# Graph network on one core: 19 and 21 of 64 tiles of source rows by matmul instead of 23 and 24

## What is computed

```python
w = relu(edgefeats @ w1 + b1) @ w2 + b2          # 400000 x 256, once
W = w.reshape(-1, 16, 16)
for _ in range(2):
    xj = hx[edge_src]                            # source rows, gathered anew in each round
    m = einsum('ei,eio->eo', xj, W)
    agg = segment_sum(m, edge_dst) / max(deg, 1)
    hx = gru_cell(agg, hx)
out = layernorm(x + hx)
```

## Time and profile before

| | |
|---|---|
| median of three runs | 6714.77 us |
| span of the profiled execution | 6694.6 us |
| around the span (median less span) | 20.2 us |
| PE busy | 5648.0 us (84%), 38360 matmuls |
| DVE busy | 4296.9 us (64%) |
| POOL busy | 3811.1 us (57%), 4006 gathers |
| ACT busy | 3179.0 us (47%) |
| granted TensorE clock, mean | 0.882 of 2.4 GHz |

### The profile page before, as it was taken

The page is one execution under the profiler, slowest core; times in us unless marked ns, Lnnn a source line. Parts: engine busy times, 40 slices in busy tenths (PEclk is TensorE's granted clock), DMA queues, the critical chain, the costliest instruction groups (busy, mean ns, idle before and its releaser), DMA issues.

```text
span 6694.6 us, 119595 instructions
## 1 busy us (share of the span) xinstructions
PE 5648.0 (84%) x38360; PEld 4666.6 (70%) x38361; DVE 4296.9 (64%) x7146; ACT 3179.0 (47%) x5259; POOL 3811.1 (57%) x4021
## 2 busy tenths in 40 slices
PE   2888888888888888888858888888888888888887
PEld 1777777777777777777647777776777777777775
DVE  3766666666666666666636666666666666666665
ACT  1554555445554545454325454454545454444442
POOL 6355555555555555555555555555555555555553
PEclk7988998889898999998878898898988889888887
DMA  4111111111111111111111111111111111111110
GB/s 107 46 34 48 34 48 34 48 34 48 34 48 44 39 48 34 48 34 48 25 47 29 40 29 40 33 37 39 31 40 29 40 29 41 29 40 29 40 29 20
DMA packets 197656, 263.32 MB, mean 39 GB/s; under 512 B 95745, under 2 KB 165942, under 8 KB 184205
## 3 DMA queue, kind: packets, MB, share of 16 engines
q1 hardware_dynamic: 61885, 216.66, 9.5%
q0 software_dynamic: 128192, 33.07, 4.8%
q10 hardware_dynamic: 7026, 6.21, 0.4%
HBM read 195.73 MB, written 54.92 MB: 37 GB/s over the span
## 4 chain that ended last, share of the span: by engine, by line
PE 65%; issue 14%; another core or an unknown queue 10%; ACT 6%; DVE 3%; DVEq 1%; DMA 0%; POOL 0%; ACTq 0%; POOLq 0%; SPq 0%
PE ps_all L722 45%; PE ps_all L732 8%; ACT src_hot L603 3%; PE ps_all L755 3%; PE ps_all L745 3%; PE ps_all L709 3%; PE ps_all L776 2%; ACT src_hot L607 2%; DVE shared L1137 1%; DVE fan L1092 1%; PE ps_all L762 0%; ACT shared L576 0%; ACT h_sb L570 0%; DVE xg L1145 0%
## 5 line engine op out<-in xcount | busy, mean ns | idle before, releaser
L722 PE MATMUL ps_all<-parts,src_hot 125*128 125x400 f32 x18048 | 3820.4, 368 | 258.7 <-issue 166.4
L722 PEld LDWEIGHTS ps_all<-parts,src_hot 125*128 125x128 f32 x18048 | 3501.9, 202 | 482.6 <-issue 367.7
L535 POOL DMA_INDIRECT xg<-in_x,idx x2027 | 1923.4, 949 | 1394.3 <-issue 556.1
L535 POOL DMA_INDIRECT xg<-h_rows,idx x1979 | 1873.1, 946 | 1371.6 <-issue 518.7
L1137 DVE TENSOR_TENSOR shared<-ps_all,at_hot 128x400 f32<-128x400 f32 x2256 | 1211.8, 566 | 1858.8 <-remote 1168.4
L603 ACT ACTIVATE src_hot<-keys,neg_key 128x384 fp32r<-128x384 int16 (+1 forms) x3072 | 1617.0, 599 | 1653.1 <-remote 979.0
L732 PE MATMUL ps_all<-fan,h_sb 128*32 128x160 f32 x12544 | 825.0, 316 | 489.5 <-issue 435.8
L1092 DVE TENSOR_TENSOR fan<-xg,ps_all 128x1280 f32<-128x1280 f32 x784 | 1158.8, 1478 | 88.0 <-DVE xg L1145 33.4
L607 ACT ACTIVATE src_hot<-src_hot 128x1536 fp32r<-128x1536 f32 (+1 forms) x768 | 1122.2, 1461 | 72.3 <-ACT src_hot L603 2.8
L1145 DVE TENSOR_REDUCE xg<-shared 128x48 f32<-128x1200 f32 (+1 forms) x768 | 1056.7, 1376 | 75.6 <-DVE shared L1137 1.0
L732 PEld LDWEIGHTS ps_all<-fan,h_sb 128*32 128x32 f32 x12544 | 391.8, 111 | 842.4 <-issue 794.9
(11 more groups left out here) (120 smaller groups left out, 1383.7 us busy)
## 6 DMA issues: line engine op xcount, KB each, us to landing
keys<-key_d SPq DMA_DIRECT2D x96, 768.0 KB
h_d<-h_sb SPq DMA_DIRECT2D x49, 1056.0 KB
h_sb<-h_d SPq DMA_DIRECT2D x49, 1056.0 KB
xg<-in_x,idx POOLq DMA_INDIRECT x2027
xg<-h_rows,idx POOLq DMA_INDIRECT x1979
ef<-in_ef_t SPq DMA_DIRECT2D x49, 420.0 KB
acc_all<-agg_t SPq DMA_DIRECT2D x1, 3161.0 KB
idx<-in_src_tiles SPq DMA_DIRECT2D x98, 32.0 KB
```

The costliest lines, as they stand in the source:

```text
L535: pool.indirect_dma_start(out=xg[:, buf, at, 0:C], out_offset=None, in_=rows_of, in_offset=bass.IndirectOffsetOnAxis(ap=idx[:, buf, at:at ...
L722: last = pe.matmul(ps_g[j], src_hot[0:KP, k % 2, kb, j * P:(j + 1) * P], parts[0:KP, m, kb, :], start=(kb == 0 and m == 0), stop=(kb == KB ...
```

## The change

Two rows of numbers. In round 0 steps 1, 2, 4 and 6 go from 3 tiles by PE to 2 (sum 23 to 19). In round 1 steps 0, 1 and 4 do (24 to 21). POOL gathers 45 and 43 tiles of a super instead of 41 and 40. The buffers and tables of `keys`, `at_pe` and `at_hot`, sized by the larger number of each step, shrink from 24 tiles to 21.

```diff
-BY_PE = ((2, 3, 3, 3, 3, 3, 3, 3), (3, 3, 3, 3, 3, 3, 3, 3))
+BY_PE = ((2, 2, 2, 3, 2, 3, 2, 3), (2, 2, 3, 3, 2, 3, 3, 3))
```

## The result

The changed kernel takes 6956.9 us, median of 4 runs (6954.7 to 6963.8), against 6715.4 us, median of 4 runs of the kernel before: ratio 1.0371, 95% interval 1.0348 to 1.0394. Forecast was 6215 us. It is slower by 242 us, not faster by 500.

What follows compares the result with a forecast made beforehand. PE with its stutters was taken to bound the kernel; -530 (tiles) -20 (ACT) +40 (DVE) +10 (round starts) gave -500 us, so 6215 us from 6715, with a range of 6110 to 6450 us.

Steps and rivals of the forecast that it cites:

- I put the steady state at nothing: POOL's 336 added gathers, 420 us more work, were to hide in its idle time and cost 0 us.
- The free step boundary of rows 6: On POOL, a step boundary was read to cost nothing when its wait is already fulfilled: the same 0.30 us of idle.
- PE with its stutters sets the pace: PE, 84% busy and stuttering with no named wait, was taken as the bound on a super of about 66 us.
- -530 us for the tiles: PE loses 4 and 3 tiles a super over 47 supers in each round: 510 to 555 us gained, taken as 530.
- +40 and -20 us of hand-offs: 40 us lost to PE's waits for DVE's picks, 20 us gained from shorter waits for ACT's one-hots.
- The cover of 24 us for each gather: Gathers run 24 us ahead of the PE products that use their rows, so one more gather, 1.25 us, was covered.
- Slower: POOL already sets the pace: Rival, chance 0.06: POOL's own step cost fills its idle time, so added gathers cost 411 us: 7126 us.
- the 376 waits: POOL's waits for an update of unknown maker, 782.9 us in all, taken as waits for PE's `products`.
- Price by number: Rival, chance 0.18: PE's instructions cost by number, about 84 ns each: 6273 us; a skill-page price gave 326 us saved.
- hand-offs: Rival, chance 0.13: half of the 500 us returns as waits for picks and one-hots: 6465 us; sign, over 150 us.
- more gained: Rival, chance 0.10: PE's stutters fall with its instruction count, 65 us, plus the tiles' upper end: about 6115 us.
- L722 at 15360: Sign of being right: 15360 PE matmuls on that line, a super about 60 us, POOL's waits for PE some 700 us.

Runs made afterwards that it cites:

- long set: Runs on one chip where the kernel before, unedited, takes 6712 to 6761 us (medians).
- y3_no_gathers: Kernel before, but from super 2 on POOL issues no gathers (those rows are left out of the sums): 5170.0 us, ratio 0.7708.
- short sets: The two sets of runs, each on its own chip, where the kernel before, unedited, takes 5146 and 5151 us.
- x4_lead8: Kernel before with LEAD 8 instead of 4, where the kernel before takes about 5.15 ms: 5144.3 us, ratio 0.9997.
- z3_pause: Kernel before, but POOL waits after every step until its own gathers have landed: 6928.7 us, ratio 1.0254.

## Why the prediction was wrong

**The step that failed: "I put the steady state at nothing"** for 336 added gathers. Alone they cost 447 us in a long set and 415 us in a short one: 1.33 and 1.24 us each, where gathers back to back start 1.25 us apart. The arithmetic took POOL's 14.8 us idle in a super for free room. It is not free: it is eight pauses of about 2 us, one behind every burst, and a longer burst does not eat its pause but lengthens it (2.03 us behind five gathers, 3.04 behind ten). The free step boundary of rows 6 was read rightly, but a burst that ran on through it was paid for by the 3.54 us wait behind it, in the very next row shown.

**The premise behind it, "PE with its stutters sets the pace",** was half right. PE was the engine waited for (a lead of eight changed nothing), but its work was not what took the time: in `y3_no_gathers` the same tiles take 51 us a super in round 0 and 48 in round 1 (median distance of its `products`), not 66. 84% busy hid this, for PE's recorded time is itself longer with gathers, 5670.6 us at a granted clock of 0.878 against 4913.8 us at 0.973 without.

**-530 us for the tiles** was mis-sized for that reason. Thinning alone, the one half of the change, gave 195 us, ACT's and DVE's hand-offs included; a little over a third of the term. PE had less to do in each step, but the burst of five with its pause still took 8.15 us.

**+40 and -20 us of hand-offs** were not measured apart. The waits of L722 for picks and one-hots are 156.1 us together in the profile after, over the 150 us named as the mark; they are more likely a sign of held completions than of slow picks: a pick takes 566 ns before and 568 after.

**The cover of 24 us for each gather was right**: `fan` waited for gathers four times, 28.9 us in all, PE waited for `fan` 93.7 us, under the mark of 100, and a gather still takes 947 ns. That is why the lead looked safe. Lateness of rows was never the price.

**The rivals.** "Slower: POOL already sets the pace" had the sign and the price (411 us; 447 measured), at 0.06, and asked the right question of the 376 waits. It gave 7126 us since it allowed PE's thinning nothing; with the 195 us it would have come to 6931 us. That would have been luck in part, for its mechanism, POOL's own cost at a step, holds only in the short sets, in its plainest form (no idle at all, each gather at its spacing); in the long ones the lead of eight speaks against it. Price by number, hand-offs and more gained all shared the failed step. The sum of the last, -555 - 20 + 40 + 10 - 65, gives 6125 us and not 6115. The estimate of 326 us in the first rival takes a price for a matmul for weight loads too: for the 2632 matmuls alone it would be half. No run here shows that price, and no chance was built on it. Of the marks named, "L722 at 15360" came, "a super of about 60 us" did not (70.3 and 67.3), POOL's waits for PE by name shrank to 441.0 us, but those for the unknown maker grew to 912.4: the sum, 1353, should have been near 700.

The Trainium skill, "SBUF — State Buffer" (SBUF: two separate sides), has some DVE operations lock out the writing of GpSimd's descriptors, which the prediction let stand as a possible help to this rival. No run here shows it: the gather's median is 947 ns before and after, and in `x4_lead8`, with DVE 83% busy, gathers run unbroken at 1.248 us. Whether any DVE operation of this kernel takes that lock the runs don't tell.

What is shown for the long sets: the indirect gathers, and not as many plain transfers, their queue or a POOL busy with memsets, lengthen the run by 1542 us; added gathers cost 1.33 us each; stutters lie in and behind the long bursts and nearly vanish (62 to 111 us) where POOL is made to stop behind each step. But in those three kernels POOL became the bound, so that less was asked of PE too. Argued from the order of events only: that the gathers hold up PE's updates. The pause of POOL itself ends with such an update, so that waits end in pauses doesn't say which of the two holds the other; the runs without gathers say that gathers are at the root, not how. Open: why the kernel before takes 5.15 ms in two sets of runs, with none of these waits, and 6.7 ms in the others. Each chip had one set only, so that it goes with the chip is likely but not shown.

## What to carry to other kernels

Idle time of an engine in short equal pieces, one behind each burst of its work, is a cost of that work until shown otherwise: price added work by the period (burst and pause together, here 8.2 us for five gathers), not by the busy time that would fit in. When an engine is over 80% busy and still stutters without a named wait, lay its stutters over the bursts of the others before calling its work the bound; one run with the suspect left out (here 1542 us) tells more than the whole arithmetic. And time both kernels in more than one set of runs, on more than one chip: here the balance of two engines was another in some.

## What was not expected of the hardware

- In one burst, an update of PE for DVE came 9 us late while POOL gathered back to back, and PE slowed to a matmul each 0.7 to 1.4 us from 7 us into it. Of 935 us of stutters before, 841 lie in bursts of 9 to 12 gathers and the pauses behind them.
- The same kernel took 6712 to 6761 us (medians) in four sets of runs and 5146 and 5151 us in two, with the gather at 0.947 us in both kinds.
- A memset of 0.33 us with a drain, between two gathers, cost POOL 2.5 us; a plain transfer of the same 128 rows costs it 0.53 us, an indirect one 0.95 us.
- A POOL that waited for the landing of its last gather (`z3_pause`) went on 2.24 us after that gather's end, at the median of 783 such stops.
